# Normalized rows turned by transfers instead of TensorE, the FFN a stage later, the result formed by an adding transfer

## What is computed

```
u = (x - mean_c) / sqrt(var_c + 1e-6)                     # over the 96 channels
patches = 3 x 3 patches of u                              # 16*32*32 of them, 9 columns of 96 channels
y = patches . w_mask / (|patch column| |w_mask|)          # 512 prototypes; best column and prototype by argmax
integrate = best column * sim + prototype * (1 - sim)
h  = leaky_relu([integrate, 9 sims] @ w_i1.T + b_i1);  vcs = tanh(h @ w_i2.T + b_i2)
h2 = relu(vcs @ w_l1.T + b_l1) @ w_l2.T + b_l2;        x = x + (w_conv applied to h2's 9 positions)
t  = x as tokens of 96 channels
n  = (t - mean) / sqrt(var + 1e-5)
FFN: q_mul rounds to 5 exponent and 2 mantissa bits, q_acc to float16
f  = relu(q_acc(q_acc(q_mul(n) @ q_mul(W1).T) + q_mul(b1)))
out = t + q_acc(q_acc(q_mul(f) @ q_mul(W2).T) + q_mul(b2))
```

## Time and profile before

| | us |
|---|---|
| median of three runs | 1992.98 |
| the profiled execution's own time | 1996.22 |
| its span, first to last instruction | 1994.4 |
| PE busy in the span | 1898.1 (95%) |
| DVE busy | 1866.6 (94%) |
| ACT busy | 1656.4 (83%) |
| POOL busy | 1621.8 (81%) |
| granted clock of PE, mean | 0.985 |

### The profile page before, as it was taken

The page is one execution under the profiler, slowest core; times in us unless marked ns, Lnnn a source line. Parts: engine busy times, 40 slices in busy tenths (PEclk is TensorE's granted clock), DMA queues, the critical chain, the costliest instruction groups (busy, mean ns, idle before and its releaser), DMA issues.

```text
span 1994.4 us, 44820 instructions
## 1 busy us (share of the span) xinstructions
PE 1898.1 (95%) x13105; PEld 1429.9 (72%) x13105; DVE 1866.6 (94%) x6525; ACT 1656.4 (83%) x3205; POOL 1621.8 (81%) x1170
## 2 busy tenths in 40 slices
PE   5899999999999999999999999999999999999964
PEld 3567777777777777777777777777777777777642
DVE  7999999999999999999999999999999999999740
ACT  1168888888888888888888888888888888888885
POOL 2578888888888888888888888888888888888752
PEclk9999999999999999999999999999999999999985
DMA  3324545454454545445454454544545455454322
GB/s 96 100 73 129 135 125 147 117 147 125 134 139 117 150 122 139 133 127 145 116 147 126 129 143 117 146 126 133 139 119 151 118 143 129 122 150 118 92 74 71
DMA packets 83890, 249.78 MB, mean 125 GB/s; under 512 B 15736, under 2 KB 17986, under 8 KB 83650
## 3 DMA queue, kind: packets, MB, share of 16 engines
q1 hardware_dynamic: 52866, 170.80, 27.3%
q0 software_dynamic: 28672, 75.52, 18.0%
q10 hardware_dynamic: 2112, 0.60, 0.2%
HBM read 133.23 MB, written 57.02 MB: 95 GB/s over the span
## 4 chain that ended last, share of the span: by engine, by line
PE 72%; DVE 10%; issue 6%; ACT 5%; POOL 3%; DMA 2%; POOLq 0%; SPq 0%; ACTq 0%; DVEq 0%
PE y_ps L648 11%; PE y_ps L650 11%; PE y_ps L649 11%; PE bank L673 9%; PE bank L703 8%; PE bank L685 6%; PE bank L739 4%; ACT y L475 4%; PE bank L754 3%; PE bank L713 3%; DVE best_y L1025 3%; PE bank L723 2%; POOL prod L390 2%; DMA wsel<-proto_rows,w_index 1%; PE bank L711 1%
## 5 line engine op out<-in xcount | busy, mean ns | idle before, releaser
L475 ACT CAST y<-bank 128x384 f16<-128x384 f32 x1152 | 554.1, 481 | 185.9 <-PE bank L673 175.4
L1025 DVE TENSOR_REDUCE best_y<-y_ps 128x2 f32<-128x1024 f32 (+1 forms) x640 | 704.6, 1102 | 0.6 <-PE y_ps L650 0.6
L648 PE MATMUL y_ps<-proto_hi,xh 96*128 96x512 f32 x1152 | 574.1, 498 | 22.5 <-DVE best_y L1025 15.1
L483 ACT ACTIVATE h<-y,f_b 128x1152 f16<-128x1152 f16 x384 | 471.7, 1270 | 0.0
L649 PE MATMUL y_ps<-proto_lo,xh 96*128 96x512 f32 x1152 | 456.5, 396 | 0.0
L650 PE MATMUL y_ps<-proto_hi,xl 96*128 96x512 f32 x1152 | 455.9, 396 | 0.0
L673 PE MATMUL bank<-tqt,f_w 96*128 96x384 f16 x1152 | 390.2, 339 | 42.4 <-ACT y L475 34.7
L411 POOL TENSOR_TENSOR xl<-xc,xh 96x1152 fp32r<-96x1152 f32 x128 | 341.2, 2666 | 26.4 <-ACT xh L538 15.5
L343 POOL DMA_INDIRECT xsel<-x_pm,x_index x128 | 121.6, 950 | 230.0 <-DVE xn L983 216.4
L673 PEld LDWEIGHTS bank<-tqt,f_w 96*128 96x128 f16 x1152 | 110.9, 96 | 262.9 <-issue 144.4
L648 PEld LDWEIGHTS y_ps<-proto_hi,xh 96*128 96x128 f32 x1152 | 221.7, 192 | 84.1 <-issue 39.7
(11 more groups left out here) (131 smaller groups left out, 3874.7 us busy)
## 6 DMA issues: line engine op xcount, KB each, us to landing
xc<-x_cm SPq DMA_DIRECT2D x128, 432.0 KB
xp<-x_pm SPq DMA_DIRECT2D x128, 432.0 KB, 5.4
h<-h POOLq DMA_DIRECT2D x128, 432.0 KB, 4.5
out<-o_pm SPq DMA_DIRECT2D x128, 432.0 KB
xsel<-x_pm,x_index POOLq DMA_INDIRECT x128, 3.7
wsel<-proto_rows,w_index POOLq DMA_INDIRECT x128
proto_rows<-proto SPq DMA_DIRECT2D x1, 384.0 KB, 2.7
proto<-w_mask SPq DMA_DIRECT2D x1, 192.0 KB, 3.3
```

The source lines that it names most:

```text
L475: act.copy(y16[:, q, r * TOK:(r + 1) * TOK], bank[0][:, 0:TOK]).then_inc(s_y16, 1)
L483: act.activation(h16[:, q, :], y16[:, q, :], ACT.Relu, bias=f1_b[:, q:q + 1]).then_inc(s_h16, 1)
L648: pe.matmul(y, hi, proto_hi[:], start=True, stop=False)
L1025: dve.tensor_reduce(best_y[t % 2][:, j0:j1], y_ps[n % 2][:, 0:j1 - j0, :], AX_X, ALU.max).then_inc(s_yd, 1)
```

## The change

Three things are done differently. The nine transposes by TensorE and the two copies by ScalarE are gone; SP issues nine transposing transfers from tq to tqt instead, each 128 x 128 of float16, for which tq's positions are padded to 128 columns and tqt has 128 rows and three buffers. A stage TURN stands between NORM and FFN, so FFN, FFN2 and STORE are one slot later, and there are 141 slots. And GpSimd's addition into o_pm becomes a transfer issued by GpSimd, which adds zb (float16) onto t_pm (float32) in place; the store reads t_pm, and `residual` waits for the store that last read its buffer, `ffn2_bias` for the adding transfer that last read zb. The orders of the slots on POOL, ACT, PE and DVE are also others.

```diff
-LOAD, SPLIT, MATCH, SELECT, PICK, MIX, INPUT, HIDDEN, CONV, NORM, FFN, FFN2, STORE = range(13)
+LOAD, SPLIT, MATCH, SELECT, PICK, MIX, INPUT, HIDDEN, CONV, NORM, TURN, FFN, FFN2, STORE = range(14)
...
-        tq = [sb(f"tq{b}", [P, JC], F16) for b in range(2)]
-        tqt = [sb(f"tqt{b}", [C, JP], F16) for b in range(2)]
+        tq = [sb(f"tq{b}", [P, J, P], F16) for b in range(2)]
+        tqt = [sb(f"tqt{b}", [P, JP], F16) for b in range(3)]
...
+            def turned_out(self, t):
+                self.wait(s_tx[t % 3], 16 * 9 * (t // 3 + 1))
...
# SP, in a slot: after the loads of xc and xp
+                if run.live(s, NORM):
+                    t = s - NORM
+                    sp.wait_ge(s_tq, t + 1)
+                    run.wait(s_f1, NC * (t - 2))
+                    for j in range(J):
+                        sp.dma_start(tqt[t % 3][:, j * P:(j + 1) * P], tq[t % 2][:, j, :],
+                                     transpose=True).then_inc(s_tx[t % 3], 16)
                 if run.live(s, STORE):
                     t = s - STORE
-                    sp.wait_ge(s_o, t + 1)
-                    sp.dma_start(out[t], o_pm[t % 2][:]).then_inc(s_os[t % 2], 16)
+                    run.landed(s_o, t)
+                    sp.dma_start(out[t], t_pm[t % RING][:]).then_inc(s_os[t % RING], 16)
...
# POOL, t_norm
-                    run.wait(s_tf, 2 * (t - 1))
+                    run.turned_out(t - 2)
...
# POOL, output
                     pool.wait_ge(s_zb, t + 1)
                     pool.wait_ge(s_t, 2 * (t + 1))
-                    run.landed(s_os, t - 2)
-                    pool.tensor_tensor(o_pm[t % 2][:], t_pm[t % RING][:], zb[:], ALU.add).then_inc(s_o, 1)
+                    pool.wait_ge(s_dev, t + 1)
+                    run.apart()
+                    pool.dma_start(t_pm[t % RING][:], zb[:], accum_op=ALU.add).then_inc(s_o[t % 2], 16)
...
# PE, ffn1 (and the function turn is removed)
                     if k == 0:
-                        pe.wait_ge(s_tt, 2 * (t + 1))
+                        run.turned_out(t)
...
-                              tqt[t % 2][:, r * TOK:(r + 1) * TOK], start=True, stop=True).then_inc(s_f1, 1)
+                              tqt[t % 3][0:C, r * TOK:(r + 1) * TOK], start=True, stop=True).then_inc(s_f1, 1)
...
# DVE, ffn2_bias
-                    run.wait(s_o, t)
+                    run.landed(s_o, t - 1)
...
# DVE, residual
+                    if n == 0:
+                        run.landed(s_os, t - RING)
```

More of the change, by code:

```diff
@@ L162, in build @@
         zb = sb("zb", [P, JC], F16)
-        o_pm = [sb(f"o_pm{b}", [P, JC]) for b in range(2)]
         s_mask = sem("prototypes_loaded")
@@ L212, in build @@
         s_tq = sem("tq_ready")
-        s_tf = sem("tqt_filled")
-        s_tt = sem("tqt_ready")
+        s_tx = [sem(f"tqt_turned{b}") for b in range(3)]
         s_f1 = sem("ffn1_filled")
@@ L221, in build @@
         s_zb = sem("zb_ready")
-        s_o = sem("out_ready")
-        s_os = [sem(f"out_stored{b}") for b in range(2)]
+        s_o = [sem(f"t_pm_out{b}") for b in range(2)]
+        s_os = [sem(f"out_stored{b}") for b in range(RING)]
         block = ctx.enter_context(nc.Block())
@@ L435, in slot @@
                 gather_x(s)
-                hidden8(s)
                 lock(s)
                 t_norm(s)
+                hidden8(s)
+                product(s)
                 t_center(s)
-                product(s)
                 low_x(s)
-                output(s)
                 low_h(s)
                 gather_w(s)
+                output(s)
             run.slots(slot)
@@ L492, in ffn2_out @@
                     act.copy(z16[:, j0 * C:j1 * C], bank[2 - n][:, 0:(j1 - j0) * C]).then_inc(s_z, 1)
[L494 to L501, removed]
             def squares(s):
@@ L575, in slot @@
                 ffn1_out(s, 3)
+                weighted(s)
                 mix_out(s)
+                ffn1_out(s, 4)
                 layer1_out(s)
-                weighted(s)
-                ffn1_out(s, 4)
-                turned(s, 0)
                 ffn1_out(s, 5)
-                turned(s, 1)
                 hidden1_out(s)
@@ L652, in match @@
                         last.then_inc(s_y, 1)
[L654 to L664, removed]
             def ffn1(s, k):
@@ L761, in slot @@
                 ffn1(s, 0)
+                conv(s, 0)
+                conv(s, 1)
+                ffn1(s, 1)
                 hidden2(s)
-                conv(s, 0)
                 match(s, 2)
-                ffn1(s, 1)
+                ffn1(s, 2)
                 turn_x(s)
                 match(s, 3)
-                ffn1(s, 2)
-                conv(s, 1)
                 ffn1(s, 3)
                 turn_mix(s)
-                layer1(s)
                 match(s, 4)
                 match(s, 5)
+                pick(s)
                 ffn1(s, 4)
-                turn(s, 0)
-                turn(s, 1)
+                layer1(s)
+                match(s, 6)
                 ffn1(s, 5)
-                match(s, 6)
                 hidden1(s)
                 ffn1(s, 6)
-                pick(s)
                 match(s, 7)
+                match(s, 8)
                 ffn1(s, 7)
-                match(s, 8)
                 ffn2(s, 0)
@@ L1084, in slot @@
                 x_sq(s)
-                cos(s)
+                mix_row(s)
                 x_norm(s)
-                mix_row(s)
+                best_j(s)
                 variances(s)
-                best_j(s)
+                normed_x(s)
                 root(s, 0)
@@ L1093, in slot @@
                 index(s)
-                normed_x(s)
                 root(s, 2)
@@ L1098, in slot @@
                 root(s, 4)
-                residual(s, 0)
                 root(s, 5)
                 pick_root(s)
-                ffn2_bias(s)
                 root(s, 6)
                 y_max(s, 0)
+                remainder(s)
+                residual(s, 0)
                 residual(s, 1)
                 t_mean(s)
-                remainder(s)
+                ffn2_bias(s)
                 y_max(s, 1)
+                y_max(s, 2)
+                best_v(s)
+                sims(s)
+                v_index(s)
+                y_max(s, 3)
+                y_max(s, 4)
                 x_stats(s, [0, 1, 2])
                 x_stats(s, [3, 4])
-                y_max(s, 2)
                 x_stats(s, [5])
                 x_stats(s, [6, 7, 8])
-                sims(s)
-                best_v(s)
-                y_max(s, 3)
-                v_index(s)
-                y_max(s, 4)
             run.slots(slot)
```

15 lines of the change are left out of this document (8 added, 7 removed).

## The result

The changed kernel takes 3011.18 us (median; 3005.56 to 3011.6), the kernel before 1992.55 in the same comparison: ratio 1.5085, 95% interval 1.505 to 1.5119. The forecast was 1982 with a range of 1966 to 2110. It is wrong in sign and far outside the range. In a few executions (two of e11's six, one of e12's six, one of the kernel before beside e1 to e4) the chip ran in a slower state: the ratios leave them out, the medians don't, and e11's trace is of such a one.

What follows compares the result with a forecast made beforehand. TensorE and VectorE were taken as level, VectorE having only 0.25 us of a slot to give. From 1996.2, 21 us off the middle and 10 more for the drain gave 1985, or 1982 against the median; range 1966 to 2110.

Steps and rivals of the forecast that it cites:

- The change removes nothing from VectorE: it puts its instructions in another order.: Middle slots: VectorE keeps its 14.39 busy us a slot and has only 0.25 us of idle time to give.
- Its instructions have steady durations, so this is work: VectorE from 200 to 1840 us: its 1612.0 busy us of 1640 were taken as work.
- That is the cap of any gain in the middle: Middle slots: VectorE's idle 0.25 us a slot limits any gain there to 1.7%.
- the four cases: Forecast 0.54, nothing gained 0.15, DMA engines or SP fill up 0.18, adding transfer lands late 0.13.
- The chosen threshold, 1.44 an issue: SP's queue: from 1.44 us for each of nine transposing issues, SP itself sets the slot.
- the third case: DMA engines or SP's queue fill up: slower, 2195 at 0.75 us a turn, 2840 at 1.31; chance 0.18.
- The sum of 11.2 in 14.4: DMA engines: existing 7.2 us a slot plus 2.2 for the adding transfer and 1.8 for nine turns, of 14.4.
- L = 5: The adding transfer lands 5 us after its issue; ffn2_bias is not held up below 8.0.
- the fourth case: Adding transfer lands late, holding ffn2_bias on VectorE beyond L = 8.0: 2040 at 8.5, 2120 at 9.2; chance 0.13.
- Nothing is lost: h8, issued after tq at 8.7, lands by 16.2 if it takes 7.5 us; TensorE may lag 2 us.
- Filling costs nothing: First slots: the extra stage adds no time there, since the matching, which has not moved, sets early slots.
- The Forecast case: All three kinds of transfer hidden, VectorE loses most idle time: 1982 against the median, range 1968 to 1990; chance 0.54.

Runs made afterwards that it cites:

- e11: e10 with one transposing transfer a tile over all nine positions instead of nine; 2161.74 us, ratio 1.0788 to the kernel before.
- e12: e11 with GpSimd's hidden8 back ahead of lock, so h8's transfer is issued before tq's calculation; 2111.05 us, ratio 1.0533.
- e1: The changed kernel with only ffn2_bias back in its old place, between pick_root and root 6; 2239.73 us, ratio 1.1224.
- e4: The changed kernel with ffn2_bias's addition replaced by a 16-bit copy of z16, leaving FFN2's bias out; 2979.42 us, ratio 1.4924.
- e2: The kernel before with only ffn2_bias moved behind t_mean, its place in the changed kernel; 2810.56 us, ratio 1.4078.
- e17: e14 with nine transposing transfers a tile instead of one; 2176.03 us, ratio 1.088 to the kernel before.
- e14: e12 with SP's order changed: loads of xc and xp first, then the store of the tile before, then the turn; 1991.71 us, ratio 0.998.
- e13: e10 with GpSimd's hidden8 back ahead of lock, nine transposing transfers a tile; 2219.76 us, ratio 1.1098.
- e10: e1 with two buffers of zb, the adding transfer's landing awaited two tiles later, all nine turns; 2241.38 us, ratio 1.1233.
- e7: The kernel before with the adding transfer alone, two zb buffers, the store a slot later behind the loads; 1995.72 us, ratio 1.0005.
- e6: The changed kernel with only GpSimd's low_h moved from behind low_x to behind product; 2638.68 us, ratio 1.3227.
- e15: e14 with GpSimd's addition into o_pm, behind gather_w, instead of the adding transfer, and one zb; 2165.12 us, ratio 1.0848.
- e16: e15 with GpSimd's addition back in its old place, between low_x and low_h; 2089.93 us, ratio 1.047.

## Why the prediction was wrong

**The step that failed: "The change removes nothing from VectorE: it puts its instructions in another order."** The order was taken as free, "Its instructions have steady durations, so this is work" was read from a kernel in which none of them met GpSimd in this way, and "That is the cap of any gain in the middle" had no counterpart for a loss. ffn2_bias was placed at 9.2 in the text's own time, the roots' end at 7.0 with tq from there: both times stood under one heading, so GpSimd's calculations could be seen to lie under the moved line. What was missing is the question which of VectorE's instructions had until then run only beside GpSimd's idle time or its issues. Measured in its place: ffn2_bias lasts 6.57 us longer a tile, worth 771 us (e1), and it does so without the rest of the change too (e2). No rival covered it, and the four cases together had given it no share.

**SP and the nine turns.** The estimate of 0.6 us an issue was the row nearest in form; one takes 1.23 undisturbed, nine 12.07, and beside other transfers nine take 13.3 to 15.7 (e1, 1000 to 1300 us). The chosen threshold, 1.44 an issue, was right: undisturbed they fit below it, and loaded (1.60 in e17) SP sets the slot. So this part of the third case did happen, as the second cost behind the first. By place: 184 us (e14 to e17), 109 (e12 to e13), 80 (e11 to e10). The row of the Trainium skill (VectorE: DVE Perf Modes, § The three transpose paths), 1309 ns for one, is near the issue time in a row, 1232 ns; it can't be read as engine time, since the turns' queue grew by only 1.7 us of 16 engines a tile: 25.4% of 3009.3 us for it after, 27.3% of 1994.4 on the page before, over 128.

**The DMA engines.** 1.8 us for nine turns was close to that 1.7, and 2.2 for the adding transfer to its 2.0 (20.3% of 3009.3 less the 18.0% of 1994.4 in the earlier trace rows, over 128). The sum of 11.2 in 14.4, 0.78, is what e14 shows: 0.77. The engine half of the third case didn't come.

**The adding transfer.** L = 5 was forecast; it lands 3.8 us after its issue in the changed kernel and 4.6 in e7, and ffn2_bias waits for it for 5.7 us of the whole span. So the fourth case didn't come. Forecast was too that the loads slide behind it, harmlessly, and "Nothing is lost" by h8's later issue. Here the two were held apart in the text, each with its own deadline, and their meeting was not: h8 issued together with store and loads lands after 7.7 us instead of 4.1 (e12, e14). In the changed kernel itself, with its long slots, it still lands after 4.2. Loads first is worth 119 us with one turning instruction (e12 to e14) and 44 with nine (e13 to e17); h8 ahead of tq 51 and 22.

**The sum where its conditions hold.** e14 has all three parts of the change (turns by transfer, the extra stage, the adding transfer) and none of the faults above, so its time can be held against the forecast's terms. By the issues of xc, slot 13 starts at 166.6 us before and at 179.8 in e14; the last load at 1831.2 and 1820.4; the spans are 1994.4 and 1993.9. The 114 slots between take 1664.6 and 1640.6: 24.0 us less, forecast 21 (0.21 a slot of the 0.25, for which 0.18 was taken). What follows takes 163.2 and 173.5: 10.3 more, forecast 10. Its parts are near too: the extra slot 11.8 (12 taken; 1964.25 to 1976.09 by ffn2_bias), the end behind the last zb 1.6 (2.6 taken), which leaves -3.1 for the shorter drain slots (-4.5 taken).

The slots before slot 13 take 13.2 more, where "Filling costs nothing" stood. 12.3 of that come between slots 3 and 8 (54.6 us before, 66.9 in e14), where VectorE is busy as long (53.7 and 53.3) but waits for the matching for 11.9 us instead of 0.6. Before, x_stats stood between the y_max calls; in the new order it comes behind them all. e7, with the old orders and the adding transfer, takes 54.6 as well, and the first turn is issued only in slot 9. So it is the new orders, and that it is x_stats among them is argued, not tested.

Together, -24.0 + 10.3 + 13.2 is 0.5 us less. In the medians e14 gains 4.3 us, 0.2%, so a change without fault would have given less than half of the forecast's 11. The Forecast case weighed a gain of 10 us against three conditions which, when unmet, cost 771, 184 and 119 us in the runs above.

**How the loss adds up** (medians; the parts depend on their order): 3011 to 2240 by ffn2_bias's place, 2241 to 2220 by h8's, 2220 to 2176 by the order of the loads, 2176 to 1992 by one instruction for nine.

## What to carry to other kernels

When a change reorders an engine's instructions, lay VectorE's new order beside GpSimd's calculations and mark each VectorE instruction that works from SBUF to SBUF: one that lands in an unbroken run of GpSimd can cost the rest of that run, not one instruction (a reduction of one tile was not held up here). Count DMA instructions per queue, each with the issue time of its own kind, since a queue can be full before the DMA engines are: here SP's was, with the engines at 0.72. One instruction over nine blocks took about a seventh of nine. A transfer that replaces a calculation turns a short wait into a landing of about 4 us, so see what is queued behind that wait and with which transfer it will then start.

## What the runs showed of the hardware that I had not expected

- A 128x864 float16 addition or copy on VectorE, 0.60 us alone, took 7.1 to 7.7 us beside four GpSimd calculations in a row (e2 and the changed kernel), counted as busy. In the slots shown it was let in neither at the boundaries between them nor during the 0.64 us of h8's issue; in e6 it was let in early in some slots. Instructions as small as 128x9 float32 (148 ns) wait too, 1.4 us in the mean (e15).
- A reduction of one float32 tile in SBUF is not held up (1.05 us beside a calculation of GpSimd, 1.03 without).
- A transposing transfer of 128x128 float16 within SBUF holds SP's queue for 1.23 us undisturbed and about 1.6 in the mean beside other traffic, where some take up to 2.3 and the rest still 1.23 (e1, the nine at 1199.52); nine blocks in one instruction hold it for 1.5 (e16), 1.8 (e11), 1.9 (e14) or 2.7 us (e12) in the median, and take 2.2 us of 16 engines (in e14: 41.3% of 1993.9 us less 27.3% of 1994.4, over 128).
- A transfer that adds 128x864 float16 into float32 took GpSimd 0.87 to 1.03 us to issue (h8's, which casts, 0.59) and landed after 3.8 (changed kernel), 4.6 (e7) and 5.3 us (e14) in the median.
- TensorE's granted clock fell to 0.80 in the middle of the changed kernel, where TensorE was busy for 72% of the time: a mean of its two levels, 1.2 GHz (0.50) and 2.4 GHz (1.00). In e14, with TensorE busy for 98%, it was 1.00.
